# Storing the forms of x1 as rows and transposing them in the DMA load

## The reference

```python
x1 = layernorm(x + attention(x))          # 32 query heads, 8 key/value heads, head size 32, rotary, causal
y  = (silu(x1 @ gate_w.T) * (x1 @ up_w.T)) @ down_w.T    # 3584 hidden; ternary weights times a scale per row
out = layernorm(x1 + y)
```

## Time and profile before

| | |
|---|---|
| median of 3 runs | 2036.66 us (2034.21 to 2037.75) |
| profiled execution, its own time | 2036.07 us |
| its span in the trace | 2034.3 us |
| TensorE busy | 1904.2 us, 94% |
| VectorE, ScalarE, GpSimd busy | 60%, 39%, 25% |
| DMA traffic | 189.78 MB, 93 GB/s over the span |

### The profile page before, as it was taken

One profiled execution on the slowest core, in us unless ns is written; L12 is line 12 of the kernel. 1 busy time (PEld: TensorE's weight loads), 2 busy tenths in 40 slices (PEclk: granted clock), 3 DMA queues, 4 the chain that ended last, 5 costly groups with the idle time before them and its releaser, 6 DMA issues.

```text
span 2034.3 us, 30091 instructions
## 1 busy us (share of the span) xinstructions
PE 1904.2 (94%) x11680; PEld 954.0 (47%) x11680; DVE 1226.8 (60%) x2156; ACT 792.0 (39%) x1190; POOL 510.4 (25%) x935
## 2 busy tenths in 40 slices
PE   4999999999999997887999999999789999999995
PEld 1665655555556553343444444444334444444442
DVE  5877777678766775444545444457844444444468
ACT  4254434434543443436433433433144334334320
POOL 1154446445544553322000000002500000000026
PEclk7999999999999998899999999999999999999998
DMA  6202012202220234435321321325432213213112
GB/s 234 64 12 58 13 48 89 79 20 92 74 79 12 91 129 137 155 128 192 134 93 52 104 93 52 104 102 209 176 105 94 93 52 104 93 52 104 63 53 93
DMA packets 92478, 189.78 MB, mean 93 GB/s; under 512 B 41136, under 2 KB 41392, under 8 KB 92336
## 3 DMA queue, kind: packets, MB, share of 16 engines
q1 hardware_dynamic: 91472, 187.46, 27.2%
q10 hardware_dynamic: 864, 0.39, 0.1%
HBM read 147.71 MB, written 39.85 MB: 92 GB/s over the span
## 4 chain that ended last, share of the span: by engine, by line
PE 83%; DMA 5%; DVE 5%; POOL 3%; issue 2%; ACT 2%; SPq 1%; ACTq 0%; DVEq 0%; POOLq 0%
PE bank L836 32%; PE bank L729 17%; PE bank L850 17%; PE bank L788 4%; PE bank L776 3%; PE bank L751 3%; PE bank L799 2%; PE bank L740 2%; PE bank L754 1%; PE bank L807 1%; DMA att_parts<-att_spill 1%; DMA x_forms_spill<-x_form_made 1%; DVE stats L1081 1%; DVE last_down L1176 1%; DMA row<-x 1%
## 5 line engine op out<-in xcount | busy, mean ns | idle before, releaser
L836 PE MATMUL bank<-x_forms,weight_forms 128*128 128x512 f16 x3136 | 718.6, 381 | 25.3 <-DVE gate_blocks L1134 12.1
L836 PEld LDWEIGHTS bank<-x_forms,weight_forms 128*128 128x128 f16 x3136 | 306.9, 98 | 401.3 <-issue 24.1
L850 PE MATMUL bank<-w_down,hid 128*128 128x512 f16 x1792 | 422.4, 380 | 12.2 <-DVE last_down L1176 11.8
L899 ACT ACTIVATE p_tiles<-bank 128x512 f32<-128x512 f32 (+1 forms) x352 | 193.2, 557 | 319.7 <-PE bank L776 318.6
L850 PEld LDWEIGHTS bank<-w_down,hid 128*128 128x128 f16 x1792 | 174.2, 98 | 229.2 <-DVE last_down L1176 20.2
L1237 POOL TENSOR_TENSOR acc<-acc,down_scale 128x1024 f32<-128x1024 f32 x16 | 38.8, 2427 | 932.0 <-DVE acc L1172 932.0
L1020 DVE TENSOR_REDUCE row_max<-bank 128x1 f32<-128x384 f32 (+3 forms) x352 | 218.7, 635 | 73.9 <-PE bank L754 71.6
L729 PE MATMUL bank<-wq_parts,xT_parts 128*128 128x256 f16 x1536 | 224.2, 274 | 8.7 <-DVE wq_parts L971 8.5
L729 PE MATMUL bank<-wo_parts,att_parts 128*128 128x512 f16 x768 | 198.2, 385 | 10.3 <-DMA att_parts<-att_spill 6.7
L1205 POOL TENSOR_SCALAR_AFFINE_SELECT p_tiles<-p_tiles 128x128 f32<-128x128 f32 (+2 forms) x352 | 136.0, 393 | 252.3 <-ACT p_tiles L899 251.6
L1172 DVE TENSOR_TENSOR acc<-bank,acc 128x512 f32<-128x512 f32 x160 | 110.3, 689 | 130.3 <-PE bank L850 130.3
(11 more groups left out here) (106 smaller groups left out, 2026.6 us busy)
## 6 DMA issues: line engine op xcount, KB each, us to landing
w_page<-gateT SPq DMA_DIRECT2D x56, 512.0 KB, 4.8
w_page<-upT SPq DMA_DIRECT2D x56, 512.0 KB, 4.4
w_page<-downT SPq DMA_DIRECT2D x56, 512.0 KB, 4.6
x_forms_spill<-x_form_made SPq DMA_DIRECT2D x56, 256.0 KB, 2.2
x_forms<-x_forms_spill SPq DMA_DIRECT2D x56, 256.0 KB, 6.1
att_spill<-att_made SPq DMA_DIRECT2D x64, 128.0 KB, 2.1
att_parts<-att_spill SPq DMA_DIRECT2D x16, 512.0 KB, 3.3
x_row<-x_spill SPq DMA_DIRECT2D x16, 512.0 KB, 3.6
```

The costliest lines, as they stand in the source:

```text
L836: t = nc.tensor.matmul(strassen[to][:, :], w_form[:, use % 4, A_FORMS[a_form], k * P:(k + 1) * P], xF[:, :, B_FORMS[b_form], col:col + P], ...
L850: t = nc.tensor.matmul(to[:, :], hid[q % 2][:, c, a, i % 2, i // 2 * P:(i // 2 + 1) * P], w_down[:, q % 2 * GC + c, cols], start=c == 0 an ...
L899: nc.scalar.activation(p32[j][:, h0:h0 + heads, :], bank[5 + m % 2][:, 0:heads * n].rearrange("p (h c) -> p h c", c=n), ACT.Exp, scale=SCO ...
```

## The change

The forms are stored as they are made, as rows of tokens, and the load transposes them. `x1_tr` and `x1_copy` go, with their semaphores and the buffer `xF_s`. The store reads `x1_p` itself. As `x1_p` is one buffer, `x1_hi` of the next form now waits until the store of the form before has landed. The loads are the same 56, of the same bytes, each as one `dma_start_transpose` of a 128 x 1024 float16 array.

```diff
-        put(SC, at, .65, "x1_hi", pair, form, after=there + ([] if first else [("x1_tr", *before)]))
+        put(SC, at, .65, "x1_hi", pair, form, after=there + ([] if first else [("xF_store", *before)]))
         put(VE, at, .8, "x1_lo", pair, form, after=[("x1_hi", pair, form)])
-        put(PE, at, .5, "x1_tr", pair, form, takes="T",
-            after=[("x1_lo", pair, form)] + ([] if first else [("xF_store", *before)]))
-        put(SC, at, 1.05, "x1_copy", pair, form, frees="T", after=[("x1_tr", pair, form)])
-        put(SY, at, .1, "xF_store", pair, form, lands=2.4, after=[("x1_copy", pair, form)])
+        put(SY, at, .1, "xF_store", pair, form, lands=2.4, after=[("x1_lo", pair, form)])
...
-    xF_dram = nc.dram_tensor("x1_forms_spill", [TILES // 2, NPR, P, KD * P], F16, kind="Internal").ap()
+    xF_dram = nc.dram_tensor("x1_forms_spill", [TILES // 2, NPR, P, 2 * HALF], F16, kind="Internal").ap()
...
-        xF_s = sb(A, "x1_form_made", [KD * P], F16)
...
-                elif kind == "x1_tr":
-                    on.wait_ge(s_x1lo, made_n[which] + 1)
-                    trans_free((kind, *which))
-                    to = tb.rearrange("p (h c) -> p h c", h=KD)
-                    for a, k in itertools.product(range(2), range(KD // 2)):
-                        t = nc.tensor.transpose(to[:, a * (KD // 2) + k, :], x1_p[:, a, k * P:(k + 1) * P], idH[:, :])
-                    t.then_inc(s_x1tr, 1)
...
                 elif kind == "x1_hi":
                     before_form(on, *which)
-                    on.wait_ge(s_x1tr, made_n[which])
+                    on.wait_ge(s_xF, 16 * made_n[which])
                     nc.scalar.activation(x1_p[:, 0, :], x1_form_of(*which), ACT.Copy, scale=X1_UP).then_inc(s_x1hi, 1)
-                elif kind == "x1_copy":
-                    on.wait_ge(s_x1tr, made_n[which] + 1)
-                    on.wait_ge(s_xF, 16 * made_n[which])
-                    nc.scalar.activation(xF_s[:, :], bank[TRANS][:, :].bitcast(F16), ACT.Copy).then_inc(s_x1c, 1)
...
                 elif kind == "xF_store":
                     pair, form = which
-                    on.wait_ge(s_x1c, made_n[which] + 1)
-                    e.dma_start(xF_dram[pair, B_FORMS[form]], xF_s[:, :]).then_inc(s_xF, 16)
+                    on.wait_ge(s_x1lo, made_n[which] + 1)
+                    e.dma_start(xF_dram[pair, B_FORMS[form]], x1_p[:, :, :].rearrange("p a c -> p (a c)")).then_inc(s_xF, 16)
...
-                    e.dma_start(xF[:, pair, i, :], xF_dram[p * PAIRS + pair, i]).then_inc(s_xF_in[i], 16)
+                    e.dma_start_transpose(xF[:, pair, i, :].rearrange("p (c t) -> p c t", c=KD),
+                                          xF_dram[p * PAIRS + pair, i]).then_inc(s_xF_in[i], 16)
```

More of the change, by code:

```diff
@@ L558, in block_kernel @@
         s_x1 = [sem(f"x1_store_dma{i}") for i in range(2)]
-        s_x1hi, s_x1lo, s_x1tr, s_x1c = sem("x1_hi"), sem("x1_lo"), sem("x1_transposed"), sem("x1_copied")
+        s_x1hi, s_x1lo = sem("x1_hi"), sem("x1_lo")
         s_x1f, s_xF = sem("x1_form"), sem("x1_form_store_dma")
@@ L582, in block_kernel @@
         NFIRST = 2 * KD
-        trans = [(k, w) for k, w in plan.order[PE] if k in ("stack_tr", "max_tr", "sums", "x1_tr")]
+        trans = [(k, w) for k, w in plan.order[PE] if k in ("stack_tr", "max_tr", "sums")]
         trans_n = {(k, *w): n for n, (k, w) in enumerate(trans)}
@@ L590, in block_kernel @@
         made_n = {w: n for n, (k, w) in enumerate([p for p in plan.order[SC] if p[0] == "x1_hi"])}
-        for engine, kind in ((VE, "x1_lo"), (PE, "x1_tr"), (SC, "x1_copy"), (SY, "xF_store")):
+        for engine, kind in ((VE, "x1_lo"), (SY, "xF_store")):
             assert [w for k, w in plan.order[engine] if k == kind] == list(made_n), kind
@@ L692, in trans_free @@
                         on.wait_ge(s_mcopy, which[0] + 1)
-                    elif kind == "sums":
+                    else:
                         on.wait_ge(s_scale_att, 4 * (which[0] * UG + which[1]) + 1)
-                    else:
-                        on.wait_ge(s_x1c, made_n[which] + 1)
             tb = bank[TRANS][:, :].bitcast(F16)
```

## The result

The changed kernel takes 2046.77 us (median of 5 runs, 2046.3 to 2052.13) against 2037.75 us (5 runs, 2034.21 to 2040.21) for the kernel before beside it: a ratio of 1.0051 [1.0034, 1.0068], 0.5% slower. The forecast was 2031 us, 0.3% faster; the time lies in the range, on the other side of no change. The profiled execution took 2046.3 us with a span of 2044.6, 10.3 us above the span before.

What follows compares the result with a forecast made beforehand. It took TensorE, busy 94% of the span, as the bound. From 2036.07 us, -14.4 - 2.3 - 6.4 - 3 + 4 + 14.7 + 2 = -5.4 gave 2030.7, as a median 2031 us; range 2010 to 2056.

Steps and rivals of the forecast that it cites:

- The terms for what goes: TensorE's transposes go: -14.4 us up to 762 us, -2.3 to 840, -6.4 after; their waits go: -3.
- The rival of the filler: TensorE's transposes were only filler, so half of the 23 us comes back: 2042 us, chance 0.12.
- The term of +4 us for `x1_hi`'s wait: ScalarE in attention: 20 us of extra waits for store landings, a fifth reaching TensorE; bounds 0 and 20.
- The rival that this wait decides the time outside the burst: `x1_hi` in attention delays exponentials, replacing TensorE's removed work: slower, 2047 us at the bound; chance 0.13.
- The first burst, +14.7: First-pass loads on SP's queue take 33.5 us, lengthening ScalarE's and TensorE's stall by 14.7 us; bounds 0 and 132.
- The test that the prediction named: Sign of being right: a burst's 28 loads land over 31 to 37 us, TensorE's stall there near 27.
- The second burst, +2: Second pass: `last_x1` behind the loads on SP's queue comes late for VectorE; +2 us, bounds 0 and 5.
- Plain speed: Both bursts: transposing loads are as fast as plain ones; -22 us, 2015 us, chance 0.20.
- Small pieces or blocks: Both bursts: loads cost by small piece (151 us each, 2262 us) or by block (some 2540 us); chance 0.10.
- a sign of being wrong: First burst: the stall is no longer than now because another order of SP's queue lets the store pass.

Runs made afterwards that it cites:

- experiment 1: Changed kernel with its 56 transposing loads made plain again, order of all engines kept: 2019.31 us, 0.9903.
- experiment 8: Changed kernel with first-pass loads planned at 1.35 us, second-pass loads ranked later, and `x1_p` doubled: 2017.93 us, 0.9893 (2012.9 us without the doubling).
- experiment 3: Changed kernel with the first pass's 28 transposing loads put together to four of 128 x 7168: 2040.25 us, 1.0010.
- Experiment 4: Changed kernel with a first-pass load counted as 1.35 us of SP's queue in the plan instead of 0.1: 2019.01 us, 0.9903.
- Experiment 10: Changed kernel with loads planned at 1.35 us (first pass) and 1.5 us (second pass), second-pass loads ranked later: 2008.49 us, 0.9857.
- 12: Experiment 10 with its 56 transposing loads made plain, order of all engines kept: 1997.69 us, 0.9800.

## Why the prediction failed

**The error as a whole.** The traces differ by +10.3 us where the sum has -5.4. Of these 15.7 us the second burst has 12.0, the first 4.4, the rest of the terms takes off 1.5, and 0.8 come behind the last event.

**The terms for what goes: right in mechanism and in size.** The stage up to the first burst is 13.9 us shorter (said: 14.4). From the stall's end to the second pass it gains 9.7 us, where the prediction had 2.3 + 6.4 + 3 = 11.7, or 7.7 with the 4 us for ScalarE's landings taken off; how the 9.7 divides over the first three was not tried by itself. The rival of the filler is refuted by this and by experiment 1: it has half of some 23 us coming back, and the traces gain 23.6 us of the 26.1 counted.

**The term of +4 us for `x1_hi`'s wait** was too much. ScalarE did wait for landings: 72.9 us in the kernel after, 36.1 of them in the burst. But up to the burst 17.2 us of such waits left TensorE's waits for exponentials where they were (1.1 us), that stage gained 13.9 of its 14.4 us, and experiment 8 takes 50 us of such waits away and gains nothing. The rival that this wait decides the time outside the burst is refuted. In the burst that wait is the link through which the stall comes, as forecast; that the chain goes on through `x1_lo` and the sums in TRANS, where before it went through the copy, was not foreseen.

**The first burst, +14.7: right mechanism, too small.** It cost 19.1 us. The value was taken from the attention store's 256-byte pieces, 219 GB/s; the loads ran at 195 GB/s, one every 1.35 us and not every 1.2, and held the queue for 37.9 us and not 33.5. The 4.4 us between these are the 4.4 us of the error, so the working itself held: the burst's time less that of the same data at the plain rate, 18.8 us. The test that the prediction named (a burst between 31 and 37 us, a stall near 27) was passed over by a little: 37.9 and 32.5.

The Trainium skill, DMA: Bandwidth & Descriptors, section Latency and other measured facts, has 261 GB/s for DMA transposes not contiguous in a middle dimension; by it the burst would be 28 us. The trace disagrees for 28 narrow loads (195 GB/s) and comes near it for four wide ones (265 GB/s, 27.97 us, experiment 3). Both kinds of load read whole contiguous rows, so the condition of that figure may not be met here, and the nearness may be chance.

**The second burst, +2: the step that failed.** It cost 14.0 us, nearly three times its upper bound of 5. The prediction had the right place (`last_x1` behind the loads) and the right consequence, and three things were off.

*How long the queue is held.* It was held from 1399.25 to 1441.44, 42.2 us, where the text had some 32 (1403.79 to about 1436). That alone makes the first row 10 us later than forecast. Of the 10 us, 4.4 are the first burst's error over again. 1.3 are a slip: the text added 14.7 us to the time at which the queue was free before, but 33.5 us of loads from 1403.79 on end at 1437.3. The other 4.3 are the row load between the two groups of loads (0.6) and three long loads. The median of a load is 1.31 us here too, but the mean from one to the next is 1.48 (41.46/28). One load took 3.06 us, right behind two weights pages; one 1.79 us, while that row was landing; and one 2.70 us, while almost no data moved for some 1.8 us (from 1420.9). What lengthened them was not tried, and weights do not explain the last: from 1408 to 1440 us 24,019 of 24,042 packets are under 512 bytes.

*The next row.* VectorE waited 5.21 us for it in place of 2.87. It was issued 1.6 us after the row before it had been used (before: 1.4), but took 6.6 us to land and not 4.4. The DMA engines were fully busy from 1442 to 1452 us with pages and an output that had been issued behind the burst; that these slowed the row is likely and was not tried.

*The bounds.* 0 and 5 were worked out from the value taken for the first burst and not from its ends (19 to 151 us), so an uncertainty that was written down one paragraph earlier was lost.

With the burst's held time right in both places the same working would have given +19.1 and about +12 (1446.0 + 4.4 against 1439.37, and 1 for the next row), and a forecast of some 9 us slower.

**The other rivals.** Plain speed: refuted, a load holds the queue for 1.35 us against 0.48; experiment 1 shows what that rival would have been worth, 2019 us against 2015 said. Small pieces or blocks: refuted, a burst is 38 us and not 151. (Its 115 us at the second burst should have been 120 by its own rows; no conclusion changes.) Eight 128x128 blocks in 1.31 us are 0.16 us a block in a stream. The Trainium skill, VectorE: DVE Perf Modes, section The three transpose paths, gives 1309 ns for one; no trace shows a single one alone, and for blocks in a stream that figure is eight times what the trace has.

**What was not on the list.** The queue's order as a free choice. That the plan counts a load at .1 us was written down, and another order that lets the store pass was named as a sign of being wrong, but no rival or chance was made of it: the burst was taken as given. Experiment 4 shows that the sign of this change hung on that number: 1.0051 with .1, 0.9903 with the measured price, where the kernel before with its own measured price has 0.9951. Experiment 10, which also prices and ranks the second pass's loads, comes to 0.9857.

## What to carry to other kernels

Work that is moved onto an in-order queue is priced by what it holds up, not by its own lateness: list who stands behind it and how soon each is needed, at every place where the queue bursts, and carry the uncertainty of the price to each of them. When a planner fixes the order, give it the new measured price in the same change; here that was worth 30 us for a change that by itself lost 10. Then give the same correction to the old kernel too, before crediting the change with it (19 us of the 29 remained).

## What the runs showed of the hardware

- A transposing load of 128 x 1024 float16 holds SP's queue 1.31 us (median in both bursts), against 0.43 us for a plain one. From one load to the next it is 1.35 us in the first burst, against 0.48, and 1.48 in the second, where three loads took 1.8 to 3.1 us. It lands 3.8 us after issue (median). The next instruction of the queue waits, also one that needs nothing of it.
- Its data goes in packets of about 250 bytes: 195 GB/s at 128 x 1024 a load, 265 at 128 x 7168 with 290 inside a load, and 4.6 to 6.6 us for 1 MB at 128 x 4096. What sets the last was not settled.
- At the same 187 GB/s the DMA engines are 91% busy with transposing loads and 59% with plain ones in their place (experiments 10 and 12).
